# A mixture-of-experts kernel: the row scatters of the second half of the tokens follow each other without a memset and a wait between them

## What is computed

```python
x = x + jnp.tanh(g_xattn[0]) * _L0_xattn_ref(ctx_512, _layernorm(x, axis=-1), L0_xattn_W, L0_xattn_b)
x = x + jnp.tanh(g_ffn[0]) * _L0_ffn_ref(_layernorm(x, axis=-1), ...)
# in _L0_ffn_ref:
combine = jnp.zeros((T, E), dtype=x.dtype).at[jnp.arange(T)[:, None], topk_idx].add(topk_w)
g = jnp.einsum('th,ehm->etm', xf, gate_w)
u = jnp.einsum('th,ehm->etm', xf, up_w)
eo = jnp.einsum('etm,emh->eth', jax.nn.silu(g) * u, down_w)
routed = jnp.einsum('te,eth->th', combine, eo)
shared = jax.nn.silu(xf @ sh_gate_w) * (xf @ sh_up_w) @ sh_down_w
```

## Time and profile before

| | |
|---|---|
| median of 3 runs | 258.53 us (258.03 to 259.87) |
| profiled execution | 258.77 us, span 256.9 us |
| PE busy | 219.3 us (85%) |
| POOL busy | 157.4 us (61%) |
| DVE busy | 129.4 us (50%) |
| ACT busy | 80.0 us (31%) |
| L432 scatters, 48 | 47.5 us |
| L445 adds, 56 | 86.7 us |
| DMA queues: SP's, POOL's, ACT's | 41.7%, 35.7%, 5.9% of 16 engines |

### The profile page before, as it was taken

How to read it: one execution, slowest core, us unless ns; L and a number is a source line. 1 busy time by engine, 2 the same in 40 slices (tenths; PEclk the granted TensorE clock), 3 DMA queues, 4 the chain that set the end, 5 groups by cost and what they waited for, 6 DMA issues and landing times.

```text
span 256.9 us, 5093 instructions
## 1 busy us (share of the span) xinstructions
PE 219.3 (85%) x1043; PEld 170.9 (67%) x1044; DVE 129.4 (50%) x528; ACT 80.0 (31%) x222; POOL 157.4 (61%) x188
## 2 busy tenths in 40 slices
PE   7996987994799789999999999999999998996000
PEld 6895776882677467877777777778777776774000
DVE  2898886929554444434443444434343443343334
ACT  3636121011010124343434344344444433442000
POOL 6352888787878873528468488566575665475300
PEclk9779799997599999999999999999999999999555
DMA  6999999999997649999998768777667675257767
GB/s 200 250 260 278 407 376 331 332 373 292 318 351 255 195 151 337 253 303 214 249 231 158 126 112 154 121 121 119 107 117 108 110 119 81 35 64 153 175 168 260
DMA packets 41018, 53.72 MB, mean 209 GB/s; under 512 B 5134, under 2 KB 35438, under 8 KB 40998
## 3 DMA queue, kind: packets, MB, share of 16 engines
q1 hardware_dynamic: 25520, 30.99, 41.7%
q0 software_dynamic: 11280, 18.36, 35.7%
q10 hardware_dynamic: 4198, 4.15, 5.9%
HBM read 31.72 MB, written 21.77 MB: 208 GB/s over the span
## 4 chain that ended last, share of the span: by engine, by line
PE 61%; DVE 17%; DMA 8%; issue 5%; another core or an unknown queue 4%; POOL 4%; ACT 1%; SPq 0%; ACTq 0%; POOLq 0%; DVEq 0%
PE pG L742 26%; PE pY L756 18%; PE pX L736 5%; DMA sum_dram<-xnT,idx 5%; PE pH L750 5%; PE pG L765 3%; PE pY L692 2%; PE pY L784 2%; DMA wgu<-sum_dram 2%; POOL rows_dram L432 1%; DMA wij<-in_L_xattn_W_dram 1%; PE pH L773 1%; DVE wgu L1013 1%; POOL rstd L418 1%
## 5 line engine op out<-in xcount | busy, mean ns | idle before, releaser
L445 POOL DMA_INDIRECT sum_dram<-xnT,idx x56 | 86.7, 1548 | 57.2 <-ACT xnT L559 30.8
L742 PE MATMUL pG<-wgu,sdown 128*128 x224 | 75.8, 461 | 1.4 <-issue 1.4
L432 POOL DMA_INDIRECT rows_dram<-rows,row_i x48 | 47.5, 989 | 18.3 <-issue 11.3
L756 PE MATMUL pY<-wd,sup 88*128 x224 | 57.5, 379 | 0.0
L1134 DVE COPY sup<-pH 88x256 f32<-88x256 f32 x56 | 23.5, 420 | 59.0 <-PE pH L750 51.3
L742 PEld LDWEIGHTS pG<-wgu,sdown 128*128 128x128 f32 x224 | 38.5, 191 | 13.9 <-issue 2.0
L559 ACT ACTIVATE xnT<-pY,wt 128x256 f32<-128x256 f32 x56 | 26.5, 473 | 54.1 <-issue 22.4
L756 PEld LDWEIGHTS pY<-wd,sup 88*128 88x128 f32 x224 | 38.0, 190 | 3.2 <-issue 0.2
L750 PEld LDWEIGHTS pH<-ident,sgate 128*88 128x88 f32 x112 | 18.0, 161 | 13.6 <-DVE sgate L1130 0.5
L552 ACT ACTIVATE sgate<-pG 128x176 f32<-128x176 f32 x56 | 17.8, 317 | 27.1 <-PE pG L742 26.0
L547 ACT ACTIVATE sdown<-pX 128x256 f32<-128x256 f32 x56 | 21.0, 377 | 4.9 <-PE pX L736 4.5
(11 more groups left out here) (183 smaller groups left out, 246.2 us busy)
## 6 DMA issues: line engine op xcount, KB each, us to landing
wgu<-in_L_ffn_gate_w_dram SPq DMA_DIRECT2D x8, 704.0 KB, 10.0
wgu<-in_L_ffn_up_w_dram SPq DMA_DIRECT2D x8, 704.0 KB, 13.0
wd<-in_L_ffn_down_w_dram SPq DMA_DIRECT2D x8, 640.0 KB
sum_dram<-zeros POOLq DMA_DIRECT2D x3, 1152.0 KB
wgu<-sum_dram SPq DMA_DIRECT2D x12, 256.0 KB, 3.9
xg<-rows_dram SPq DMA_DIRECT2D x16, 144.5 KB
rows<-rows_dram ACTq DMA_DIRECT2D x16, 144.5 KB
rows_dram<-zeros SPq DMA_DIRECT2D x8, 289.0 KB, 4.5
```

Source lines behind the costliest of these rows:

```text
L432: pool.indirect_dma_start(rows_dram[:, :], bass.IndirectOffsetOnAxis(ap=row_i[:, j, k:k + 1], axis=0), lines[:, j * ROW:j * ROW + LINE], N ...
L445: pool.indirect_dma_start(sums_dram[into[s]][:, :], bass.IndirectOffsetOnAxis(ap=idx[:, s:s + 1], axis=0), y[s], None, compute_op=ALU.add) ...
L742: ins = nc.tensor.matmul(pG[par][:, 0:2 * M].rearrange("t (g m) -> t g m", g=2), xT[:, par, k, :], wgu[:, bass.ds(e, 1), :, k, :].rearrang ...
L756: ins = nc.tensor.matmul(pY[par][:, 0:H], hT[0:MI, par, i, :], wd[:, bass.ds(e, 1), i, :], start=(i == 0), stop=(i == I - 1))
```

## The change

The memset, and POOL's wait for it, stay behind the scatters of the first half (j < JH). In the second half they are left out.

```diff
@@ -431,7 +431,8 @@
                 done = s_scat if j < JH else s_rest
                 pool.indirect_dma_start(rows_dram[:, :], bass.IndirectOffsetOnAxis(ap=row_i[:, j, k:k + 1], axis=0),
                                         lines[:, j * ROW:j * ROW + LINE], None).then_inc(done, 16)
-                chain(pool.memset(wj_wide[:, :], 0.0))
+                if j < JH:
+                    chain(pool.memset(wj_wide[:, :], 0.0))
```

## The result

The changed kernel takes 278.29 us (median of 4 runs, 276.08 to 278.98), where the kernel before took 259.20 beside it (258.03 to 260.07): a ratio of 1.0725, with a 95% interval of 1.0645 to 1.0806. It is 7% slower, and the forecast of 258.5 us was wrong. The profiled execution has 278.75 us and a span of 276.9, so the span grew by 20.0 us.

A forecast was written before the change was run, and what follows sets the result against it. PE was taken to bound the kernel, with 61% of the span and nearly full expert tiles. The change on the chain summed to 0 (-0.16 at most), so from the median 258.53 it predicted 258.5 us, range 256.8 to 260.6.

The forecast's parts named there:

- The step: Start-to-start time of POOL's second-half scatters: 1.477 us before, forecast 1.18, bounded by 0.97 and 1.27.
- The pause vanishes: Rival "The pause does not vanish": transfers hold POOL's scatters, so steps stay 1.48 us; same time, 258.5 us; chance 0.10.
- Landing and first add: POOL's second-half scatters land by 98.0, at most 6.1 us after issue; first add near 100.2, some 4.9 us sooner.
- Who was waiting: Three possible gainers from the 4.9 us: second-half tile loads, slots of the adds, the adds' queue; each worth 0.
- the first of the three: Tile loads needing the second half, first tile 12 on ACT at 108.93; landing already earlier, so worth 0.
- cover of 4.1 us: Before the change, the second-half landing at 104.8 came 4.1 us ahead of ACT's load of tile 12.
- the price of lost cover for tile 0: With the cover of tile 0's load gone, each us of its lateness would be one us of the end.
- What the denser stream costs others: Scatters put 1.25 times the bytes per us on DMA for 28 us; weights and tile loads have cover; worth 0.
- The slower rival: Denser scatters lengthen two unnamed chain pieces, perhaps code fetch; doubled, 3.2 us more, 261.7 us, or 266.8 with clock fall; chance 0.10.
- the stall is gone: The 3.16 us of unnamed pieces, perhaps from POOL's semaphore updates or a chance meeting, vanish: 255.3 us; chance 0.07.
- The range: Total time 256.8 to 260.6 us, set by the 3.16 us on the chain and the scatter of runs.
- the unknown piece: The 3.16 us of two unnamed chain pieces between 81.42 and 85.16, allowed half gone or two thirds more.

The follow-up runs named there:

- g1: The changed kernel run again unaltered, beside the kernel before: 251.64 us (two runs), 0.985 by the medians.
- e4: Changed kernel plus a short memset behind each second-half scatter, for which POOL does not wait: 250.56 us, 0.9817 of the kernel before.
- e2: Changed kernel with the pause put back for the first 12 second-half scatters, so only the last 12 lack it: 251.48 us, 0.9859 of the kernel before.
- h2: Changed kernel with the pause put back for the last 12 second-half scatters, so only the first 12 lack it: 273.19 us, 1.0555 of the kernel before.
- f8: Kernel before with the memset and its wait taken out in both halves: 280.00 us, 1.0815 of the kernel before.
- f5: The changed kernel run again unaltered, beside the kernel before: 275.71 us, 1.0656.
- h3: Changed kernel plus a short memset behind each second-half scatter, for which POOL does not wait: 277.64 us, 1.0727 of the kernel before.
- j1: Changed kernel with SP's loads of tiles 4 to 7 issued only after the second half of scatters landed: 279.56 us, 1.068 by the medians.

## Why the prediction was wrong, point by point

**The step.** I took 1.18 us, from a scatter behind another operation of POOL; it is 1.277, the upper bound (1.27), which came from the adds. The better row was the one of the same kind of instruction behind its own kind: the gap is 0.30 us between two adds and between two scatters. This miss costs 0.1 us x 23 = 2.3 us of POOL's time, and nothing of the end.

**The pause vanishes.** Right: 0.97 us per scatter, in full and in empty stretches. That rival was rightly held small.

**Landing and first add.** POOL's part held, with the start 2.6 us later (66.39 against 63.79) and the larger step. The first add was expected at 100.2 and came at 121.12, since it waits for ACT, and ACT for PE's tiles, 21.4 us late.

**Who was waiting.** "Worth 0" was right for the late condition: PE is busy 62.00 of 62.00 and 59.19 of 60.00 us behind 118. In the prompt condition the first of the three, the load of a second-half tile, was on the chain. In g1 ACT was free for it at 104.95 - 5.02 = 99.93, where it came to it at 108.93 before, and the landing took 8.00 us (6.20 in e4, 6.51 in e2), where I had 6.1 as the upper bound. So the cover of 4.1 us was worth something only as long as PE was held up ahead of it. The prediction named the price of lost cover for tile 0, but not for this.

**The failed step: "What the denser stream costs others".** I listed who shares the 16 DMA engines with the scatters, found 12 us of cover for each transfer, and wrote "Worth 0". That was right for transfers: DMA is at 0.39 in the stall. But in the late condition transfers were not all that the scatters got in the way of: with the price put at nothing, the increments became up to 18.0 us late and the first tile came 21.36 us later. With the same inventory I had two pieces of 1.53 and 1.63 us in the scatter stretch that no transfer and no engine explained. Rows of PE, DVE and ACT in the kernel before show what they were:

```profile
82.36 0.38 PE L773 MATMUL pH<-ident,sgate 128*88 128x128 f32 x2
83.45 1.35 PE L765 MATMUL pG<-wgu,xnT 128*128 128x352 f32 x4
```

```profile
83.05 0.48 DVE L1158 SCALAR_TENSOR_TENSOR xs<-pY,busy_w,xs 128x256 f32<-128x256 f32 x1 [1.62 <-remote]
85.19 0.42 DVE L1152 COPY sup<-pH 88x256 f32<-88x256 f32 x1 [1.66 <-remote]
```

```profile
87.37 0.32 ACT L563 ACTIVATE sgate<-pG 128x176 f32<-128x176 f32 x1 [2.59 <-remote]
```

PE's transposes pH ended at 82.36 + 0.38 = 82.74, DVE was free for them at 83.53, and it started on them at 85.19. PE's product pG ended at 83.45 + 1.35 = 84.80, and ACT, free by then, started on it at 87.37. To put the end of the producer beside the start of the consumer would have shown late increments of PE in the trace of before, and with that a price that may depend on how dense the scatters are.

**The slower rival (0.10).** It had the place (the busy expert's stretch), the sign, and the two pieces of 3.16 us as the thing that grows. It had the wrong cause, code fetch, and with it the wrong size: doubled, 6.3 us. They became 21.47, seven times as much, at a step shorter by a seventh. Instruction packets (q8) take 0.2% of the DMA engines' time after, and 0.3% before, and their number, 7, is the same in the changed kernel of both conditions. In the trace after, no packet of q8 stands between 53 and 103, the stretch of the stall, and the other instruction queue (q14) has one there, of 0.5 us at 90.1. The fall of the clock that it added came, though for 1.25 us beside the stall and not 5.1.

**The rival "the stall is gone" (0.07).** It fits the prompt condition, but there the stall seems gone from the kernel before too, whose times are 255 us, as the 258.5 - 3.2 = 255.3 worked out there. No edit brought that about, so it does not bear the rival out. Its reasoning, POOL's semaphore updates or a chance meeting, was nearer to the matter than code fetch.

**The range.** 256.8 to 260.6 let the unknown piece grow by two thirds. Nothing in the trace bounded its growth: it was a number without a mechanism, and I scaled it by the 1.25 of the stream. A wait whose cause is unknown has an open upper end.

## What to carry to other kernels

Before you make a stream of indirect DMAs denser, look for pieces of the chain without a name in the stretch of the stream, and compare there the end of each producer with the start of its consumer. Where the consumer was free and starts over 1 us late, the stream holds up signals, and a pause in it may be worth more than the time it takes: here 0.2 us a scatter, 4.8 us in all, kept 19 us from being lost in one condition of the chip, and cost about 1.5% in the other. And run the unaltered kernels again, at another time and on another chip, before you trust a ratio of a few per cent: the same two programs gave 1.07 and 0.985.

## What the runs showed of the hardware

- In the late condition, row scatters from POOL with a step of 1.27 us went with semaphore increments of PE up to 18 us late (product done at 79.65, ACT's start at 98.24), with all engines nearly idle but POOL and DMA at 0.39. At 1.47 us a step the largest was 1.8 to 3.2 us behind 74, at 1.73 there was none behind 66. Between 53 and 60, at 1.47 us a step, it was 2.6 to 4.7.
- Of the increments between the engines, only PE's, to ACT and to DVE, were seen late. DVE's to PE were not (82.82 to 82.88).
- Once the lateness is long, a return to 1.47 us a step did not end it before the scatters ended (h2).
- SP was slow at the same time, and it waits for nothing of PE there. It spent 19.08 us on its loads of tiles 4 to 7, against 6.62 before: `82.01 19.08 SPq L274 DMA_DIRECT2D xg<-rows_dram  x4` in the timeline of the changed kernel. Between these loads it executes register instructions. From 79 to 100.3 most of them start 0.7 us, or two or three times that, behind the one before; from 100.3 on it is 0.01 to 0.13 us. From the start of the first to that of the fourth load it is 4.6 to 5.0 us in every prompt trace, 5.2 to 6.0 in the late ones with a pause, 10.3 in f8, and 16.3 to 18.8 in the first trace of the changed kernel, f5, h2 and h3. In j1, late too, but with these loads behind the scatters, it is 4.6. So what is held up is more than PE's increments, and an account of them alone would miss SP.
- All of this was there in three of six series and in the first comparison, and not once in the other three series. A chip with one number showed both.
